# A layer's residual sum made by PE with an identity product in the output projection's bank and copied out by ScalarE, instead of added by VectorE

## The chip, the cores and the metric

The kernel runs on one core of a Trainium2 chip. The metric is the device time of one execution in microseconds (us), here the median of three runs. Engines are named as in the profile: PE is TensorE, DVE is VectorE, ACT is ScalarE, POOL is GpSimd, SP is SyncE, whose queue issues the transfers. PEld is the weight load of PE.

## What is computed

The input is 16 sequences of 512 tokens with 128 channels. Three blocks follow one another: half of a mixture of experts, a state-space block of four layers, half of a mixture of experts again.

```
x = x + 0.5 * moe(layernorm(x))          # 8 experts, width 344, top 2 of 8
x = x + mamba4(layernorm(x))
x = x + 0.5 * moe(layernorm(x))

mamba4(h):  for l in 0..3:
    xn = rmsnorm(h) * norm_w[l];  xp, z = split(xn @ Win[l])
    xc = silu(causal_conv4(xp) + conv_b);  dt, B, C = split(xc @ Wx[l])
    delta = softplus(dt @ Wdt[l] + bdt)
    state_t = exp(delta_t * A) * state_(t-1) + (delta_t * xc_t) * B_t     # 256 channels, 16 states
    y = (sum over states of state * C + xc * Dp) * silu(z)
    h = h + y @ Wblk[l]                  # the residual sum of this change
  return h @ Wout + bout
```

All of it is f32.

## The kernel before

**Tiling.** A tile is 128 partitions by 512 tokens of one sequence. The residual `h_sb` of a sequence is one such tile, channels on partitions, with four slots. The 256 inner channels are two blocks, each of them four units (j = 0..3) of four tiles: 32 scan tiles for a layer of a sequence. Such a pair of layer and sequence is called a phase, and there are 64.

**The order of work.** All engines walk over the same list of ticks t, and on each engine the instructions stand in the order of the ticks at which tables place them (`CORE`, `PREP`, `POST`, `FFN_AT`, `START`, `END`). A tick is only a place in the order: an engine goes on as soon as its semaphore waits allow. 128 ticks are a round (in the code a window, w), and in each round the core of one phase runs. Its parts, with the ticks of the round:

- ACT makes the decay exp(delta A) of each tile into one of three PSUM banks `dA_ps` (L556, every fourth tick: ..., 78, 82, 86, 90, 94, ...). An exponential waits until DVE is done with the tile three before it.
- POOL makes the input product of a unit (L909, 128x2048), DVE scans each tile (L720), and the product with C is made by POOL in pairs of tiles (L900, 128x1024, sixteen half-units for a phase less the five that DVE makes) or by DVE (L725, 128x512). PE sums over states (L405).
- In the same round PE, ACT and DVE do the preparation of the next phase (norm, convolution, projections, delta), the end of the phase before, and one expert in each 32 ticks. An expert is: PE spreads the gate (L414), DVE makes the gated input xs (L798), PE the gate projections (L421), ACT their silu (L583) in one burst with a table load before it and one behind it (L584), PE the up projections (L427), DVE the products (L805), PE the down projections (L434). The burst stands at tick 27 of each 32, so at ticks 27, 59, 91 and 123 of a round.
- An expert unit is two rounds long and begins at tick 22 of an even round. Its norm and router run in the 60 ticks ahead of that: DVE's statistics (L813, L819), ACT's normalization (L594), logits, POOL's difference of the two best logits (L930), ACT's exponential of it (L608), POOL's sum (L935), DVE's reciprocal (L855), POOL's product (L938).

**The bank s.** Five PSUM banks serve other work than the exponentials, and `s_ps` is the one that all of the preparation and the layer's end share. PE's `fill("s", ...)` waits until the last user of it is done. Ahead of the layer's end this is the copy of delta out of the bank (L684, tick 79), which itself waits for DVE's L787.

**The layer's end.** In the usual place (far; 55 of 64 phases) the output projection L514 stands at tick 83 of the round after the phase's core: two products (one for each block of `y_sb`) into `s_ps`. DVE's addition L749 stands at tick 91, behind the scan and in front of the product L725. The next layer's square L639 (`sq`) stands at tick 113. In the nine places where the next layer follows two rounds later, or after the fourth layer of one of the last two sequences (`POST_NEAR`), the projection is at tick 17 and the addition at 14. After the fourth layer `h_sb` goes into the output product (L523, L524).

```
POST = {"x1": 8, "wblk": 83, "h": 91, "attn": 105, "x2": 105}
POST_NEAR = {"x1": -65, "wblk": 17, "h": 14, "attn": 35, "x2": 56}
```

Of the kernel before, what the change touches and what calls it, by code (L numbers as in the profile page):

```python
# [8 lines left out]
ALU = mybir.AluOpType  # L9
ACT = mybir.ActivationFunctionType  # L10
# [3 lines left out]
NBLK = 2  # L14
# [21 lines left out]
NEAR = {"dc1": 98, "dc0": 84, "sq": 14, "ms": 25, "rms": 24, "xn": 27, "xp0": 45, "conv0": 42, "xp1": 47, "conv1": 53,  # L36
        "silu_xc": 59, "z0": 69, "zc0": 60, "z1": 72, "zc1": 67, "silu_z": 91, "wx": 76, "dbc": 75, "rows": 48, "dt0": 77,
        "sp0": 77, "delta0": 84, "du0": 84, "dt1": 84, "sp1": 86, "delta1": 93, "du1": 101, "dd0": 71, "dd1": 109, "bc": 55}
POST = {"x1": 8, "wblk": 83, "h": 91, "attn": 105, "x2": 105}
POST_NEAR = {"x1": -65, "wblk": 17, "h": 14, "attn": 35, "x2": 56}  # L40
FFN_AT = {"gb": 5, "xs": 2, "g0": 5, "g1": 10, "g2": 10, "burst": 5, "u0": 10, "u1": 17, "u2": 21, "hh0": 13, "hh1": 16,
          "hh2": 21, "down": 28}
START = {"load": -130, "bn": -60, "nb": -44, "xtok": -54, "xt": -38, "xT": -47, "lg": -32, "lg_sb": -35, "mx": -32,
# [18 lines left out]
PHASE = phase_table()  # L62
# [28 lines left out]
XSLOTS, HSLOTS = 2, 4  # L91
# [41 lines left out]
def post_at(t, what):  # L133

    for near, table in enumerate((POST, POST_NEAR)):
        w, s = divmod(t - table[what], W)
        if s == 0 and w - 1 in PHASE and FEEDS_NEAR[w - 1] == near:
            return ORDER[w - 1], w - 1
    return None
# [30 lines left out]
def build(nc, x, norm_w, Win, conv_w, conv_b, conv_rows, Wx, Wdt, bdt, A_log, Dp, Wblk, Wout, bout,  # L170
          Ws, bs, Wg, Wu, Wd, out, bc_rows, x1):
    with ExitStack() as ctx:
# [16 lines left out]
        wblk_sb = sb("wblk_sb", [128, NL, NBLK, D])  # L189
# [10 lines left out]
        ident = sb("ident", [128, 128])  # L200
# [16 lines left out]
        h_sb = sb("h_sb", [128, HSLOTS, T])  # L217
# [161 lines left out]
        def _(pe):  # L379
            free = {"a": None, "b": None, "s": None}  # L380

            def fill(which, sem, value):

                if free[which] is not None:
                    pe.wait_ge(*free[which])
                free[which] = (sem, value)
                return s_ps if which == "s" else ps_of[which]
# [120 lines left out]
            def post_pe(t):  # L508
                if at := post_at(t, "wblk"):
                    k, w = at  # L510
                    ps = fill("s", h_ready, k + 1)
                    for b in range(NBLK):
                        pe.wait_ge(y_gated, 2 * k + b + 1)
                        last = pe.matmul(ps[:, :], wblk_sb[:, PHASE[w][1], b, :], y_sb[:, b, :], start=(b == 0), stop=(b == NBLK - 1))  # L514
                    last.then_inc(wblk_full, 1)
                if (at := post_at(t, "attn")) and PHASE[at[1]][1] == NL - 1:
                    k, w = at
                    n = PHASE[w][0]
                    ps = fill("s", x2_ready, n + 1)
                    pe.wait_ge(h_ready, k + 1)  # L520
                    for c in range(TB):
                        o = ps[:, c * D:(c + 1) * D]
                        pe.matmul(o, h_sb[:, n % HSLOTS, c * 128:(c + 1) * 128], wout_sb[:, :], start=True, stop=False)  # L523
                        last = pe.matmul(o, ones_row[:, :].broadcast_to([1, 128]), bout_sb[:, :], start=False, stop=True)  # L524
                    last.then_inc(attn_full, 1)
# [19 lines left out]
        def _(act):  # L545
# [69 lines left out]
            def end_act(t):  # L615
# [6 lines left out]
                if (f := UNIT_OF.get(t - E * PERIOD - END["h"])) is not None and FFN[f][1] == 1:  # L622
# [3 lines left out]
                        act.wait_ge(attn_full, n - HSLOTS + 1)  # L626
                    act.activation(h_sb[:, n % HSLOTS, :], s_ps[:, :], ACT.Copy).then_inc(hin_ready, 1)

            def prep_act(t):
                if at := prep_at(t, "sq"):  # L630
                    k, w = at
# [63 lines left out]
            for t in range(FIRST, LAST):  # L695
                if t == FFN[0][0] + PERIOD:
                    act.wait_ge(w_scan, 16 * SCAN_LOADS)
                    act.activation(a_sb[:, :, :, :, :], a_sb[:, :, :, :, :], ACT.Exp).then_inc(aprep, 1)
                    act.wait_ge(aprep, 1)
                    act.activation(a_sb[:, :, :, :, :], a_sb[:, :, :, :, :], ACT.Copy, scale=-1.0).then_inc(aprep, 1)  # L700
                    for l in range(NL):
                        act.activation(win_sb[:, l, :], win_sb[:, l, :], ACT.Copy, scale=normw_sb[:, l:l + 1]).then_inc(aprep, 1)
                        act.activation(win0_sb[:, l, :], win0_sb[:, l, :], ACT.Copy, scale=normw_sb[:, l:l + 1]).then_inc(aprep, 1)
                    act.wait_ge(aprep, 2 + 2 * NL)
                core_act(t)
                burst_act(t)
                start_act(t)
                end_act(t)
                prep_act(t)

        @block.vector
        def _(dve):
# [29 lines left out]
                    dve.tensor_tensor(y_sb[:, b, :], zs_sb[:, par, b, :], y_ps[:, :], ALU.mult).then_inc(y_gated, 1)  # L742

            def post_dve(t):
                if at := post_at(t, "h"):
                    k, w = at
                    n = PHASE[w][0]
                    dve.wait_ge(wblk_full, k + 1)
                    dve.tensor_tensor(h_sb[:, n % HSLOTS, :], h_sb[:, n % HSLOTS, :], s_ps[:, :], ALU.add).then_inc(h_ready, 1)  # L749
                if (at := post_at(t, "x2")) and PHASE[at[1]][1] == NL - 1:  # L750
                    n = PHASE[at[1]][0]
                    dve.wait_ge(attn_full, n + 1)
                    dve.wait_ge(x_back[n % XSLOTS], 16 * (n // XSLOTS + 1))
                    xr = xr_sb[:, x_slot(2, n)]
                    dve.tensor_tensor(xr, xr, s_ps[:, :].rearrange("p (k d) -> p k d", k=TB), ALU.add).then_inc(x2_ready, 1)
# [279 lines left out]
```

## Time and profile before

| what | value |
| --- | --- |
| median of 3 runs | 4565.08 us (4559.62 to 4566.4) |
| the profiled execution | span 4554.2 us from its first to its last instruction; the page gives no other time for it |
| instructions | 48397 |
| busy: POOL, DVE, PE, ACT | 4093.5, 4047.9, 3939.2, 3342.2 us |
| mean granted clock of PE | 0.951 of full speed |
| chain that ended last | POOL 41%, issue 16%, DVE 14%, PE 12%, ACT 8%, DMA 3% |

The span is 10.9 us below the median of the runs. Busy times are sums over the whole span. The page's row of 40 slices shows POOL at 0 to 5 tenths in the first three slices and 6 and 0 in the last two, and at 9 tenths in every slice between.

### The profile page before, as it was taken

Reading aid. Unit: us, or ns where it says so; the run is one execution under the profiler, and the core shown is the slowest. Engines: PE = TensorE matmul, PEld = TensorE weight load, DVE = VectorE, ACT = ScalarE, POOL = GpSimd, SP = SyncE. Lnnn points to the kernel's source line nnn. Section 1 sums busy time; section 2 is a strip of 40 time slices with the busy share of each in tenths; the row PEclk is TensorE's granted clock in tenths of the full one; section 3 lists DMA queues with packets and bytes.
Section 4 is the critical chain, followed back from the end, with each engine's and each line's share of the span. In section 5 each row is a group of like instructions: output and inputs, shape, how many; then the busy total and the mean of one; then the engine's idle time right before and its main releaser. Section 6 shows DMA issues by size and latency. Waiting matters only on the chain.

```text
span 4554.2 us, 48397 instructions
## 1 busy us (share of the span) xinstructions
PE 3939.2 (86%) x11712; PEld 1280.3 (28%) x11712; DVE 4047.9 (89%) x5505; ACT 3342.2 (73%) x5047; POOL 4093.5 (90%) x1804
## 2 busy tenths in 40 slices
PE   7886777998999999899998999999899989678769
PEld 2221222232322323232232323223232323122223
DVE  2668898999999999999999999999999999889963
ACT  4566776777777777777778777777777777667734
POOL 0559999999999999999999999999999999999960
PEclk9897887999999999999999999999999999789969
DMA  2233544354434444544454445444444554444410
GB/s 72 61 78 95 115 106 98 85 118 110 97 87 112 107 93 99 114 104 96 98 112 96 97 101 119 95 97 101 112 92 89 117 113 91 101 99 95 99 41 5
DMA packets 154562, 434.46 MB, mean 95 GB/s; under 512 B 16429, under 2 KB 53230, under 8 KB 153903
## 3 DMA queue, kind: packets, MB, share of 16 engines
q1 hardware_dynamic: 154287, 431.36, 41.4%
q8 instruction: 103, 1.69, 0.2%
q14 instruction: 172, 1.41, 0.1%
HBM read 150.28 MB, written 12.58 MB: 36 GB/s over the span
## 4 chain that ended last, share of the span: by engine, by line
POOL 41%; issue 16%; DVE 14%; PE 12%; ACT 8%; DMA 3%; SPq 2%; DVEq 0%; ACTq 0%; POOLq 0%
POOL work L909 21%; POOL work L900 19%; DVE work L720 5%; DVE dA_ps L720 4%; SPq L363 2%; PE d_ps L434 2%; PE s_ps L481 2%; DVE work L725 2%; DMA bc_sb<-bc_rows 2%; ACT sg_sb L583 2%; ACT L583 1%; PE b_ps L427 1%; ACT dA_ps L556 1%; DMA dd_sb<-dd_src 1%; ACT L584 1%
## 5 line engine op out<-in xcount | busy, mean ns | idle before, releaser
L909 POOL TENSOR_TENSOR work<-dd_sb,bc_sb 128x2048 f32<-128x2048 f32 x512 | 2319.6, 4531 | 72.4 <-DMA dd_sb<-dd_src 72.2
L556 ACT ACTIVATE dA_ps<-dd_sb,a_sb 128x512 f32<-128x512 f32 x2048 | 1369.2, 684 | 643.1 <-DVE work L725 542.9
L900 POOL TENSOR_TENSOR work<-work,bc_sb 128x1024 f32<-128x1024 f32 x704 | 1655.9, 2359 | 35.1 <-DVE work L720 34.7
L720 DVE TENSOR_TENSOR_SCAN work<-dA_ps,work 128x512 f32<-128x512 f32 x1408 | 1646.7, 1203 | 40.7 <-POOL work L909 32.0
L720 DVE TENSOR_TENSOR_SCAN dA_ps<-dA_ps,work 128x512 f32<-128x512 f32 x640 | 780.9, 1220 | 10.9 <-ACT dA_ps L556 5.1
L434 PE MATMUL d_ps<-sg_sb,wd_sb 128*128 128x512 f32 (+1 forms) x1536 | 721.0, 601 | 18.8 <-DVE sg_sb L805 18.8
L405 PE MATMUL y_ps<-work,sel_sum 128*32 128x512 f32 x4096 | 580.3, 640 | 81.9 <-POOL work L900 53.7
L421 PE MATMUL a_ps<-xT_sb,wg_sb 128*128 128x512 f32 (+1 forms) x768 | 439.5, 655 | 87.1 <-ACT sg_sb L583 80.7
L421 PE MATMUL b_ps<-xT_sb,wg_sb 128*128 128x512 f32 (+1 forms) x768 | 434.5, 648 | 92.2 <-ACT sg_sb L583 87.8
L725 DVE TENSOR_TENSOR work<-dA_ps,bc_sb 128x512 f32<-128x512 f32 x640 | 435.8, 681 | 8.3
L427 PE MATMUL a_ps<-xs_sb,wu_sb 128*128 128x512 f32 (+1 forms) x768 | 412.2, 619 | 20.7 <-DVE sg_sb L805 16.2
L427 PE MATMUL b_ps<-xs_sb,wu_sb 128*128 128x512 f32 (+1 forms) x768 | 411.8, 618 | 13.4 <-DVE sg_sb L805 13.3
L434 PEld LDWEIGHTS d_ps<-sg_sb,wd_sb 128*128 128x128 f32 (+1 forms) x1536 | 279.3, 190 | 422.2 <-issue 352.7
L583 ACT ACT_TABLE_LOAD x256 | 328.4, 1283 | 85.8 <-PE d_ps L434 81.6
L805 DVE TENSOR_TENSOR sg_sb<-sg_sb,b_ps 128x512 f32<-128x512 f32 (+1 forms) x384 | 259.3, 675 | 139.8 <-PE b_ps L427 138.5
L584 ACT ACT_TABLE_LOAD x270 | 346.4, 1283 | 4.9
L805 DVE TENSOR_TENSOR sg_sb<-sg_sb,a_ps 128x512 f32<-128x512 f32 (+1 forms) x384 | 258.9, 674 | 84.5 <-PE a_ps L427 84.2
L583 ACT ACTIVATE sg_sb<-a_ps 128x512 f32<-128x512 f32 (+1 forms) x384 | 227.7, 593 | 59.4 <-PE a_ps L421 57.7
L583 ACT ACTIVATE sg_sb<-b_ps 128x512 f32<-128x512 f32 (+1 forms) x384 | 227.7, 593 | 58.5 <-PE b_ps L421 56.6
L481 PE MATMUL s_ps<-xn_pad,wconv_sb 128*128 128x512 f32 x512 | 248.9, 631 | 3.0 <-DVE xn_pad L763 2.2
L405 PEld LDWEIGHTS y_ps<-work,sel_sum 128*32 128x32 f32 x4096 | 83.0, 110 | 497.3 <-issue 359.2
L497 PE MATMUL s_ps<-dbc_sb,wdt_sb 97*128 97x512 f32 x256 | 149.5, 667 | 66.8 <-ACT dd_src L684 59.9
(116 smaller groups left out, 3823.6 us busy)
## 6 DMA issues: line engine op xcount, KB each, us to landing
dd_sb<-dd_src SPq DMA_DIRECT2D x512, 512.0 KB, 8.5
bc_sb<-bc_rows SPq DMA_DIRECT2D x256, 512.0 KB, 5.8
xr_sb<-in_L_attn_x SPq DMA_DIRECT2D x16, 256.0 KB, 3.3
bc_rows<-dbc_sb SPq DMA_DIRECT2D x128, 32.0 KB, 1.7
x<-xr_sb SPq DMA_DIRECT2D x16, 256.0 KB, 3.6
xr_sb<-x SPq DMA_DIRECT2D x16, 256.0 KB, 2.9
out<-xr_sb SPq DMA_DIRECT2D x16, 256.0 KB, 2.3
wg_sb<-in_L_ffn_Wg SPq DMA_DIRECT2D x1, 1376.0 KB
```

The costliest lines, as they stand in the source:

```text
L405: last = pe.matmul(y_ps[SEL * c:SEL * (c + 1), :], sel_sum[:, :], work[:, g % RING, c % 2, :], start=(j == 0), stop=(j == NJ - 1))
L421: pe.matmul(ps[0:fn, :], wg_sb[:, e, f0:f0 + fn], xT_sb[:, f % 2, :], start=True, stop=True).then_inc(g_full, 1)
L427: pe.matmul(ps[0:fn, :], wu_sb[:, e, f0:f0 + fn], xs_sb[:, :], start=True, stop=True).then_inc(u_full, 1)
L434: last = pe.matmul(d_ps[:, :], wd_sb[0:fn, e, ft, :], sg_sb[0:fn, ft, :], start=(e == 0 and ft == 0), stop=(e == E - 1 and ft == NFT - 1))
L556: act.activation(dA_ps[:, g % NDA, :], dd_sb[:, b, c, 0, :], ACT.Exp, scale=a_sb[:, l, b, j, c:c + 1]).then_inc(dA_ready, 1)
L583: act.activation(sg_sb[0:fn, ft, :], ps_of[job_bank(E * f + e, 1 + ft)][0:fn, :], ACT.Silu).then_inc(sg_ready, 1)
L584: act.preload_act_table_set(EXP_LN)
L720: dve.tensor_tensor_scan(dA if on_dve(i) else tile, dA, tile, 0.0, ALU.mult, ALU.add).then_inc(scanned, 1)
L725: dve.tensor_tensor(work[:, (g // 2) % RING, g % 2, :], dA_ps[:, g % NDA, :], bc_sb[:, (i // NG) % NJ, 0, :], ALU.mult).then_inc(dve_prod, 1)
L805: dve.tensor_tensor(sg_sb[0:fn, ft, :], sg_sb[0:fn, ft, :], ps_of[job_bank(E * f + e, 4 + ft)][0:fn, :], ALU.mult).then_inc(hh_ready, 1)
L900: pool.tensor_tensor(work[:, g % RING], work[:, g % RING], bc_sb[:, j, 0, :].unsqueeze(1).broadcast_to([128, 2, T]), ALU.mult).then_inc(po ...
L909: pool.tensor_tensor(work[:, g % RING:g % RING + 2].rearrange("p h c t -> p (h c) t"), dd_sb[:, b, :, 1, :], bc_sb[:, j, 1, :].unsqueeze(1 ...
```

## The change

PE puts a third product in front of the two of the output projection: the identity (`ident`, which is there already for transposes) times the old `h_sb`, accumulated in the same bank. ACT then copies the bank over the slot of `h_sb`. DVE's addition is gone. The place of the step moves from tick 91 to 85 in the usual places, so on ACT between the exponentials of ticks 82 and 86, and from 14 to 9 in the near ones; within a tick `post_act` comes behind the other parts of ACT and in front of the preparation.

```diff
-POST = {"x1": 8, "wblk": 83, "h": 91, "attn": 105, "x2": 105}
-POST_NEAR = {"x1": -65, "wblk": 17, "h": 14, "attn": 35, "x2": 56}
+POST = {"x1": 8, "wblk": 83, "h": 85, "attn": 105, "x2": 105}
+POST_NEAR = {"x1": -65, "wblk": 17, "h": 9, "attn": 35, "x2": 56}
...
                     ps = fill("s", h_ready, k + 1)
+                    pe.matmul(ps[:, :], ident[:, :], h_sb[:, PHASE[w][0] % HSLOTS, :], start=True, stop=False)
                     for b in range(NBLK):
                         pe.wait_ge(y_gated, 2 * k + b + 1)
-                        last = pe.matmul(ps[:, :], wblk_sb[:, PHASE[w][1], b, :], y_sb[:, b, :], start=(b == 0), stop=(b == NBLK - 1))
+                        last = pe.matmul(ps[:, :], wblk_sb[:, PHASE[w][1], b, :], y_sb[:, b, :], start=False, stop=(b == NBLK - 1))
                     last.then_inc(wblk_full, 1)
...
+            def post_act(t):
+                if at := post_at(t, "h"):
+                    k, w = at
+                    act.wait_ge(wblk_full, k + 1)
+                    act.activation(h_sb[:, PHASE[w][0] % HSLOTS, :], s_ps[:, :], ACT.Copy).then_inc(h_ready, 1)
...
                 end_act(t)
+                post_act(t)
                 prep_act(t)
...
             def post_dve(t):
-                if at := post_at(t, "h"):
-                    k, w = at
-                    n = PHASE[w][0]
-                    dve.wait_ge(wblk_full, k + 1)
-                    dve.tensor_tensor(h_sb[:, n % HSLOTS, :], h_sb[:, n % HSLOTS, :], s_ps[:, :], ALU.add).then_inc(h_ready, 1)
```

## Rows read from the trace of the kernel before

**Rows 1.** The page: busy us by engine; POOL's costliest group (busy, mean ns, idle before).

```profile
PE 3939.2 (86%) x11712; PEld 1280.3 (28%) x11712; DVE 4047.9 (89%) x5505; ACT 3342.2 (73%) x5047; POOL 4093.5 (90%) x1804
...
L909 POOL TENSOR_TENSOR work<-dd_sb,bc_sb 128x2048 f32<-128x2048 f32 x512 | 2319.6, 4531 | 72.4 <-DMA dd_sb<-dd_src 72.2
```

**Rows 2.** Windows view: stretch, length; busy PE, PEld, DVE, ACT, POOL; clock, DMA.

```profile
1000.00:3400.00 2400.00, 2194.18 (x6721) 717.64 (x6720) 2306.84 (x3146) 1885.95 (x2877) 2346.39 (x1035) 1.00 0.45 101
```

**Rows 3.** Waits of POOL, 1000 to 3400 us: us in total, times, longest.

```profile
POOL work L900 <- DVE work L720: 16.0, 21, 1.3
POOL wt_sb L938 <- DVE wt_sb L855: 14.0, 19, 1.1
```

**Rows 4.** Waits of DVE, the same stretch.

```profile
DVE sg_sb L805 <- PE b_ps L427: 50.4, 74, 2.9
```

**Rows 5.** Timeline of POOL: start, us, instruction, idle before it and its releaser.

```profile
590.73 2.35 POOL L900 TENSOR_TENSOR work<-work,bc_sb 128x1024 f32<-128x1024 f32 x1 [1.26 <-DVE work L720]
...
1890.58 2.36 POOL L900 TENSOR_TENSOR work<-work,bc_sb 128x1024 f32<-128x1024 f32 x1 [1.26 <-DVE work L720]
...
3855.00 2.36 POOL L900 TENSOR_TENSOR work<-work,bc_sb 128x1024 f32<-128x1024 f32 x1 [1.25 <-DVE work L720]
```

**Rows 6.** Timeline of ACT at the router's step.

```profile
1785.32 0.21 ACT L608 ACTIVATE wt_sb<-wt_sb 128x4 f32<-128x4 f32 x1 [0.34 <-POOL wt_sb L930]
```

**Rows 7.** Timeline of ACT, even round at 1829 to 1842 us.

```profile
1830.25 0.60 ACT L684 ACTIVATE dd_src<-s_ps 128x512 f32<-128x512 f32 x1 [0.59 <-DVE dd_src L787]
1830.74 1.39 ACT L556 ACTIVATE dA_ps<-dd_sb,a_sb 128x512 f32<-128x512 f32 x2
1834.53 0.69 ACT L556 ACTIVATE dA_ps<-dd_sb,a_sb 128x512 f32<-128x512 f32 x1 [2.40 <-DVE work L725]
1835.24 1.28 ACT L583 ACT_TABLE_LOAD   x1
...
1838.31 0.59 ACT L583 ACTIVATE sg_sb<-b_ps 88x512 f32<-88x512 f32 x1 [0.69 <-PE b_ps L421]
...
1840.22 1.91 ACT L556 ACTIVATE dA_ps<-dd_sb,a_sb 128x512 f32<-128x512 f32 x3
```

**Rows 8.** Timeline of DVE, the same stretch.

```profile
1836.08 0.67 DVE L749 TENSOR_TENSOR h_sb<-h_sb,s_ps 128x512 f32<-128x512 f32 x1
1836.66 0.68 DVE L725 TENSOR_TENSOR work<-dA_ps,bc_sb 128x512 f32<-128x512 f32 x1
1837.26 2.33 DVE L720 TENSOR_TENSOR_SCAN work<-dA_ps,work 128x512 f32<-128x512 f32 x2
1839.51 0.66 DVE L805 TENSOR_TENSOR sg_sb<-sg_sb,a_ps 128x512 f32<-128x512 f32 x1
1840.19 0.69 DVE L805 TENSOR_TENSOR sg_sb<-sg_sb,b_ps 128x512 f32<-128x512 f32 x1
1840.94 1.23 DVE L720 TENSOR_TENSOR_SCAN dA_ps<-dA_ps,work 128x512 f32<-128x512 f32 x1
```

**Rows 9.** Timeline of PE (matmuls), the same stretch.

```profile
1830.90 1.98 PE L514 MATMUL s_ps<-y_sb,wblk_sb 128*128 128x512 f32 x4 [0.61 <-ACT dd_src L684]
...
1833.13 1.12 PE L421 MATMUL b_ps<-xT_sb,wg_sb 128*128 128x512 f32 x2
...
1837.18 1.09 PE L421 MATMUL b_ps<-xT_sb,wg_sb 128*88 128x512 f32 x2 [0.88 <-ACT sg_sb L583]
```

**Rows 10.** Line L514, all of the span: PE's idle time before it until, us, times.

```profile
  ACT dd_src L684: 133.6, 110
```

**Rows 11.** Waits of ACT, 1000 to 3400 us.

```profile
ACT wt_sb L608 <- POOL wt_sb L930: 12.5, 17, 1.3
```

**Rows 12.** Timeline of PE at two near places.

```profile
229.99 1.98 PE L514 MATMUL s_ps<-y_sb,wblk_sb 128*128 128x512 f32 x4 [0.69 <-ACT xT_sb L605]
...
4212.80 1.13 PE L514 MATMUL s_ps<-y_sb,wblk_sb 128*128 128x512 f32 x2 [1.21 <-DVE y_sb L742]
```

**Rows 13.** Windows view of a third near place, columns as in rows 2.

```profile
4012.29:4016.07 3.78, 3.78 (x8) 1.04 (x4) 3.28 (x4) 0.20 (x1) 3.78 (x2) 0.50 0.27 101
```

## The prediction

> **What bounds the kernel now.** I read the page's busy times first. POOL and DVE are nearly equal over the span, and PE is close behind [rows 1]. An average over filling, steady work and emptying can't say which one sets the pace, so the next view is the windows view of a steady stretch: there POOL works 2346.39 of 2400 us, DVE 2306.84, PE 2194.18 and ACT only 1885.95 [rows 2]. POOL is at 97.8%. Its waits in the same stretch show what keeps it from 100%: its products (L900) wait 21 times for a DVE scan, 16.0 us, and its router step (L938) waits 19 times for DVE's reciprocal, 14.0 us [rows 3]. So POOL sets the pace, and now and then it is itself held up by a chain in which DVE comes last.
>
> The next question is what makes DVE late. DVE's own waits answer it: DVE waits for PE's up-projection, 50.4 us in 74 waits, and next to nothing for POOL [rows 4]. DVE isn't simply full; PE makes it late. I therefore followed the chain back through the timelines, starting from the longest of POOL's waits.
>
> POOL waits 1.26 us at 1890.58 for a scan. That is the tenth of the sixteen half-unit products of a phase, in an odd round (a round is 128 ticks). There are 26 odd rounds between the rows at 590.73 and 3855.00, and this same product waits over 0.1 us in 23 of them, up to 1.27 us [rows 5]. The chain behind such a wait begins some 105 us earlier, at POOL's router step L930, for which ScalarE waits (0.34 us in the row at 1785.32) [rows 6]; in between it runs through ACT, PE and DVE alone. It crosses the even round's tick 83 to 100, the place of the change, like this. ACT's exponential at 1834.53 waits for DVE's product L725 (2.40 us); behind it stand the table load, two silus, the wait for PE, a third silu, the second load and the exponentials of 1840.22 [rows 7], each starting where the one before ends. DVE's scan at 1840.94 can't start before the first of these exponentials is done [rows 8]. The old addition at 1836.08 lies in front of this scan too, but the way through ACT ends at the same time (the scan starts 0.03 us after the exponential ends at 1840.91). Two routes tie here: one over ACT's burst, and one over DVE's queue with the addition in it.
>
> **The change part by part.** *Removed:* 64 additions on VectorE, 0.67 us each. In the queue one costs 0.58 us, the distance from 1836.08 to the start at 1836.66 [rows 8]: 37 us of DVE's issue time in all, 0.58 per round.
>
> *Added on PE:* one f32 product of 128x128 by 128x512 in each phase. L514's two such products are four passes, 1.98 us, and one such product as a pair of passes is 1.12 (the row at 1833.13, same shape), so two more passes cost 0.86 us [rows 9]. The bank comes free with ACT's copy L684, and in 55 of 64 phases this copy is what L514 waits for (110 waits, weight load and product, 133.6 us) [rows 10]; the new product stands behind that same release, so it isn't hidden. In the even round: PE ends at 1830.90 + 1.98 + 0.86 = 1833.74.
>
> *Added on ACT:* a copy out of PSUM. From the start of such a copy (1830.25) to the next exponential's start (1830.74) is 0.49 us [rows 7]. There is room for it: ACT idles 2.40 us at this place. But the copy is not last in line. It is put between the exponentials of ticks 82 and 86, and it waits for PE. What is queued behind it: the exponential of tick 86, which used to run at once at about 1831.44 (the second of the pair), that of tick 90 (1834.53), and the burst. Worked out: PE's end 1833.74, plus 0.04 for the signal (PE's pair from 1837.18 ends at 1838.27 and ACT starts at 1838.31 [rows 7, 9]), copy at 1833.78; exponential of tick 86 at 1834.27; that of tick 90 another 0.62 later (three exponentials take 1.91 us, so (1.91 - 0.67)/2) at 1834.89 instead of 1834.53. **The burst starts 0.36 us later** in every round that has expert work.
>
> *Downstream of the burst.* First silu +0.36, so PE's product at 1837.18 (released by that silu) at 1837.54, the third silu, the second load and the exponential of 1840.22 at 1840.58, the scan at 1841.30. DVE, freed of 0.58, would be at its first L805 at 1838.93, but its inputs come from PE at 0.36 later than before, so DVE waits there. The gain is lost at this wait, and the chain is 0.36 longer. PE's own extra 0.86 us are absorbed earlier: PE idled 0.88 us before 1837.18 [rows 9]. The scans of ticks 95 and 99 began at 1837.26 and would be wanted at 1836.68 [rows 8]; their exponential is done at 1834.96. So no scan starves, with 1.7 us to spare.
>
> *Odd rounds.* Here DVE also carries the normalization's statistics and its queue is the later one, so the 0.58 us count for DVE, or the 0.36 count against ACT; but both end at the anchor: ACT waits for POOL's L930 in 17 of 19 cases, 12.5 us in all [rows 11]. Nothing of either reaches POOL unless ACT's reserve there, 0.34 us at the least of the usual cases, is used up. I take zero; the reserve and the 0.36 are so close that a loss here is one of the rivals.
>
> *Steady sum.* In each double round, the way from L930 to the tenth product is 0.36 us longer and POOL waits that much more. I count the 23 odd rounds that have such a wait, and nothing for the three in which POOL arrives later than the chain: 23 x 0.36 = **+8.3 us**. Bounds: from below -0.58 (DVE's way alone decides) to above 0.86 (all of PE's addition passes on) per double round.
>
> At one place the Trainium skill speaks for the change: Perfetto Trace Analysis, section Optimizing Scalar/DVE Operations, holds that when DVE is saturated, moving work to Scalar may make sense. DVE's 96% in the steady stretch looks like that case [rows 2]; by that rule the sum would be a gain of up to 0.58 us for each of 55 phases, 32 us. The waits of DVE for PE [rows 4] speak against its premise here, and my sum goes by these.
>
> *The edges.* Where few phases overlap, latency counts, and POOL waits for the load of dd_sb (72.2 us) [rows 1]. At 229.99 [rows 12] L514 waits for ACT's copy of xT: the added 0.86 is on the way, and the copy (0.60 for 0.67) gives 0.07 back: +0.8. At 4012.29 the granted clock is 0.50, the lower of its two levels, the four passes take 3.78 us [rows 13], and nothing is waited for between them: two more are +1.7, less 0.07: +1.6. At 4212.80 and two like it the second half waits 1.21 us for y_sb [rows 12], which hides the identity product, and DVE's queue is 0.58 shorter on a chain that waits for DVE: -0.6 each, -1.7 in all. The other four near places (half clock or a bank wait against a shorter queue) I put at +0.5 together. Edges **+1.2 us**.
>
> Sum +8.3 + 1.2 = +9.5. The profiled span is 4554.2 us and becomes 4563.7; the runs' median is 10.9 us above the span, and I carry that over: 4565.08 + 9.5 = **4574.6 us**, +0.21%.
>
> **The rivals.** *Faster (DVE's way decides).* If the even round's chain is limited by DVE's queue and ACT's delay has reserve, each of the 23 waits shrinks by up to 0.58 us: -13 us, 4552. For it: the addition lies on one of the two tied routes, and DVE is last before each POOL wait. Against it: the distances in [rows 7] have no slack between 1834.53 and 1840.22. It decides if the copy starts by 1833.42 (1834.53 - 0.62 - 0.49), so if PE's added product costs 0.50 us or less instead of 0.86. This is also what the skill's rule gives in sign. *No change.* POOL's waits grow in the chain but slack that I haven't seen takes 0.36 us, since the chain is 105 us long; then only the edges are left: 4566. Against: at each step that I followed the next instruction starts where the one before ends. *Every round pays.* The odd rounds use up ACT's 0.34 us in front of L608 and add to L938's wait as well: 52 x 0.36 = 18.7, with the edges 4585. For: the reserve is just the size of the delay. Against: a wait at L938 moves POOL and so shortens the following wait at the tenth product. *Starved scans.* If PE came to the product over 1.7 us later, DVE's scans would stand still for each 0.1 us beyond; this happens only in the few rounds at half clock, and would give 4590 or more.
>
> **How the numbers follow.** Forecast 0.46 (alone 4569 to 4580), faster 0.13, no change 0.22, every round pays 0.15, starved scans 0.04. The range runs from 4560, which leaves out the faster case, to 4586, which takes in the case of every round; outside are some 0.17. A measurement of this kernel tells from no change what exceeds about 0.2%, 9.1 us, so the line is at 4574.2: a little over half of the forecast's chance lies above it (0.25), with the last two 0.44 for slower; 0.43 for the same; 0.13 for faster.
>
> **What the profile after would show.** L514 with six passes and 2.84 us. ACT's copy starting 2.9 us after L514's start. The burst's table load 0.36 us later behind L684 than before (5.35 against 4.99 us from 1830.25 to 1835.24). A new wait of DVE's L805 for PE's a_ps of 0.6 us in even rounds. POOL's wait at the tenth product 0.3 to 0.4 us longer in most odd rounds, and ACT's wait at L608 in the 0.34 us cases gone. DVE's busy time 43 us less, ACT's 38 more. The prediction is wrong in its steady part if the table load comes at its old distance, or if POOL's waits for L720 fall below 34.7 us in total.

## The result, and the profile after

| kernel | median us | lowest to highest | runs |
| --- | --- | --- | --- |
| before | 4562.35 | 4557.17 to 4566.4 | 4 |
| after | 4599.16 | 4595.44 to 4602.7 | 4 |

The ratio is 1.0083, with a 95% interval of 1.0068 to 1.0097: slower by 36.8 us, where the prediction said 9.5 and its range ended at 4586. The direction was right, the size was not.

The page of the kernel after, its busy times and POOL's product with C, which answer to [rows 1], and to the products of [rows 5]:

```profile
PE 4007.3 (87%) x11840; PEld 1305.3 (28%) x11840; DVE 4019.7 (87%) x5441; ACT 3375.3 (73%) x5111; POOL 4097.1 (89%) x1804
...
L903 POOL TENSOR_TENSOR work<-work,bc_sb 128x1024 f32<-128x1024 f32 x704 | 1658.8, 2363 | 66.4 <-DVE work L728 65.6
```

DVE works 28.2 us less, ACT 33.1 and PE 68.1 us more. POOL works as long as before (4097.1 against 4093.5), in a span that is 46.8 us longer. So no engine became the bound by its work; POOL waits more. The windows view of the steady stretch says the same beside [rows 2] (same columns), where POOL had 2346.39:

```profile
1000.00:3400.00 2400.00, 2209.07 (x6706) 723.79 (x6705) 2260.37 (x3079) 1875.52 (x2867) 2314.99 (x1022) 0.99 0.44 101
```

POOL's waits in that stretch (us in total, times, longest), beside [rows 3]:

```profile
POOL work L903 <- DVE work L728: 37.8, 47, 1.5
POOL wt_sb L941 <- DVE wt_sb L858: 13.6, 19, 1.1
POOL rs_sb L920 <- DVE mv_sb L822: 10.9, 18, 0.6
```

The first was 16.0 us in 21 waits. The third is not among those of before at all: POOL's step in the normalization now waits for DVE's statistics. Both point to DVE, so the next view is DVE's own waits, beside [rows 4]:

```profile
DVE sg_sb L808 <- PE b_ps L427: 60.2, 90, 2.4
DVE y_sb L750 <- PE s_ps L515: 27.8, 36, 0.8
```

The second line names what the prediction doesn't have. L750 is DVE's gated product, y times silu(z), which writes `y_sb`. It waits for the output projection, PE's L515, which reads `y_sb`. The code says why:

```
if k > 0:
    dve.wait_ge(wblk_full, k)     # the group of the phase before has read y_sb
dve.tensor_tensor(y_sb[:, b, :], zs_sb[:, par, b, :], y_ps[:, :], ALU.mult).then_inc(y_gated, 1)
```

`wblk_full` has two waiters: the step that takes the sum out of the bank, and this product of the next phase, which must not overwrite `y_sb` while PE still reads it. For block 0 it stands at tick 87, four ticks behind the projection. The line's view, its idle time before it over the whole span (us, times), first of before, then of after:

```profile
  PE s_ps L514: 3.7, 4
```

```profile
  PE s_ps L515: 50.1, 55
```

55 is the number of phases with the usual (far) place. The timelines show one such place. Before, PE's group ended at 1830.90 + 1.98 = 1832.88 [rows 9], and DVE's queue of before stood like this (start, us, instruction):

```profile
1832.38 0.73 DVE L736 SCALAR_TENSOR_TENSOR y_ps<-xc_sb,dp_sb,y_ps 128x512 f32<-128x512 f32 x1
1833.14 0.69 DVE L742 TENSOR_TENSOR y_sb<-zs_sb,y_ps 128x512 f32<-128x512 f32 x1
1833.75 0.69 DVE L725 TENSOR_TENSOR work<-dA_ps,bc_sb 128x512 f32<-128x512 f32 x1
```

The product came 0.26 us behind the group's end, without a wait. After, the same place; PE first:

```profile
1851.25 1.12 PE L512 MATMUL s_ps<-h_sb,ident 128*128 128x512 f32 x2 [0.62 <-ACT dd_src L691]
1852.22 1.88 PE L515 MATMUL s_ps<-y_sb,wblk_sb 128*128 128x512 f32 x4
```

then DVE:

```profile
1852.73 0.73 DVE L744 SCALAR_TENSOR_TENSOR y_ps<-xc_sb,dp_sb,y_ps 128x512 f32<-128x512 f32 x1
1854.23 0.69 DVE L750 TENSOR_TENSOR y_sb<-zs_sb,y_ps 128x512 f32<-128x512 f32 x1 [0.77 <-PE s_ps L515]
1854.84 0.68 DVE L733 TENSOR_TENSOR work<-dA_ps,bc_sb 128x512 f32<-128x512 f32 x1
1855.44 0.68 DVE L801 TENSOR_TENSOR xs_sb<-xT_sb,a_ps 128x512 f32<-128x512 f32 x1
```

and ACT, beside [rows 7]:

```profile
1850.60 0.60 ACT L691 ACTIVATE dd_src<-s_ps 128x512 f32<-128x512 f32 x1 [0.59 <-DVE dd_src L790]
1851.10 0.69 ACT L557 ACTIVATE dA_ps<-dd_sb,a_sb 128x512 f32<-128x512 f32 x1
1854.13 0.60 ACT L634 ACTIVATE h_sb<-s_ps 128x512 f32<-128x512 f32 x1 [2.35 <-PE s_ps L515]
1854.63 0.69 ACT L557 ACTIVATE dA_ps<-dd_sb,a_sb 128x512 f32<-128x512 f32 x1
1855.62 0.69 ACT L557 ACTIVATE dA_ps<-dd_sb,a_sb 128x512 f32<-128x512 f32 x1 [0.30 <-DVE work L733]
1856.33 1.28 ACT L584 ACT_TABLE_LOAD   x1
```

The group ends at 1854.10. ACT's copy starts 0.03 us later, as worked out. DVE's product starts 0.13 later, and has then stood for 0.77. That number could have been read before the change: with 0.13 for the signal, the release was at 1833.01 and the product at 1833.14, a reserve of 0.13; a group 0.86 longer gives a wait of 0.73. The trace of before even holds the case itself. In one of the four waits of the gated product, PE's mean granted clock over the group was 0.66 and the four passes took 2.88 us, about as long as the six of the new group (PE, then DVE, both of before):

```profile
656.96 2.88 PE L514 MATMUL s_ps<-y_sb,wblk_sb 128*128 128x512 f32 x4 [2.28 <-ACT dd_src L684]
```

```profile
659.97 0.69 DVE L742 TENSOR_TENSOR y_sb<-zs_sb,y_ps 128x512 f32<-128x512 f32 x1 [0.81 <-PE s_ps L514]
```

Here too the product starts 0.13 us behind the group's end, and it has stood for 0.81.

What is behind it in DVE's queue moves too: the product L733, for which ACT's exponential of tick 90 waits (0.30 us), and the expert's gated input L801. The table load is now 1856.33 - 1850.60 = 5.73 us behind the copy of delta, not 4.99 as before nor 5.35 as predicted. That holds for all 36 such places between 1000 and 3400 us: 5.72 or 5.73 in each of them, against 4.98 or 4.99 before. In an odd round it goes the same way; there DVE's statistics are in the queue as well, and POOL's own step waits for them (DVE, then POOL):

```profile
1918.57 0.69 DVE L750 TENSOR_TENSOR y_sb<-zs_sb,y_ps 128x512 f32<-128x512 f32 x1 [0.77 <-PE s_ps L515]
...
1921.27 0.38 DVE L822 BATCH_NORM_AGGREGATE mv_sb<-bn_sb 128x2 f32<-128x6 f32 x4
```

```profile
1921.74 0.23 POOL L920 TENSOR_SCALAR rs_sb<-mv_sb 128x4 f32<-128x4 f32 x1 [0.58 <-DVE mv_sb L822]
```

**Where the time lies.** POOL's tenth half-unit product of a phase is again the anchor [rows 5]. Its first and last of the steady part, after:

```profile
593.97 2.37 POOL L903 TENSOR_TENSOR work<-work,bc_sb 128x1024 f32<-128x1024 f32 x1 [1.26 <-DVE work L728]
...
3899.87 2.36 POOL L903 TENSOR_TENSOR work<-work,bc_sb 128x1024 f32<-128x1024 f32 x1 [1.25 <-DVE work L728]
```

From the one to the other are 25 double rounds: 3305.9 us, against 3855.00 - 590.73 = 3264.3 before. That is 41.6 of the span's 46.8 us, 1.66 per double round; filling takes 3.2 more and emptying 1.9. Of the 41.6 us, POOL's waits for DVE's scans make 25.1 (23.5 us in 33 waits before, 48.6 in 62 after), its new wait at L920 makes 14.3 (24 waits), and one for DVE's L847 makes 3.1 (from 1.7 to 4.8); small differences take back 0.9. The tenth product itself waits over 0.1 us in 25 of the 26 odd rounds instead of 23, 31.2 us in all instead of 21.7. That is 9.5 us, under a quarter: most of the loss lies at other products and at L920.

The spans differ by 46.8 and the medians by 36.8. In every run whose span is known the time is the span plus 1.7 to 1.8 us, not 10.9, so the profiled execution of before took 6.5 us less than its median and that of after 3.5 more; sums of waits from these two traces carry this difference too.

### The profile page after: what moved, and what is told of

Its sections match the earlier page's. It is cut to its first block, busy times and chain, and to the rows that moved or that the text cites. A ratio compares the mean times of both kernels' runs of the same rounds, so it can differ in the third digit from the quotient of the medians.

```text
span 4601.0 us, 48589 instructions
## 1 busy us (share of the span) xinstructions
PE 4007.3 (87%) x11840; PEld 1305.3 (28%) x11840; DVE 4019.7 (87%) x5441; ACT 3375.3 (73%) x5111; POOL 4097.1 (89%) x1804
## 4 chain that ended last, share of the span: by engine, by line
DVE 26%; PE 18%; issue 18%; ACT 17%; POOL 16%; DMA 1%; SPq 1%; DVEq 0%; ACTq 0%; POOLq 0%
POOL work L912 9%; DVE work L728 8%; DVE dA_ps L728 8%; POOL work L903 6%; ACT dA_ps L557 4%; DVE work L733 4%; ACT L584 3%; ACT sg_sb L584 3%; ACT L585 3%; PE d_ps L434 2%; PE s_ps L481 2%; PE s_ps L515 2%; PE a_ps L421 2%; PE b_ps L427 2%; PE b_ps L421 2%
## 5 line engine op out<-in xcount | busy, mean ns | idle before, releaser
L903 POOL TENSOR_TENSOR work<-work,bc_sb 128x1024 f32<-128x1024 f32 x704 | 1658.8, 2363 | 66.4 <-DVE work L728 65.6
L728 DVE TENSOR_TENSOR_SCAN work<-dA_ps,work 128x512 f32<-128x512 f32 x1408 | 1647.7, 1205 | 41.5 <-POOL work L912 27.4
L405 PE MATMUL y_ps<-work,sel_sum 128*32 128x512 f32 x4096 | 586.3, 646 | 80.6 <-POOL work L903 47.4
L733 DVE TENSOR_TENSOR work<-dA_ps,bc_sb 128x512 f32<-128x512 f32 x640 | 437.2, 683 | 10.2
L405 PEld LDWEIGHTS y_ps<-work,sel_sum 128*32 128x32 f32 x4096 | 83.4, 111 | 503.3 <-issue 357.2
```

The lines of the kernel that those rows point to most:

```text
L405: last = pe.matmul(y_ps[SEL * c:SEL * (c + 1), :], sel_sum[:, :], work[:, g % RING, c % 2, :], start=(j == 0), stop=(j == NJ - 1))
L728: dve.tensor_tensor_scan(dA if on_dve(i) else tile, dA, tile, 0.0, ALU.mult, ALU.add).then_inc(scanned, 1)
L733: dve.tensor_tensor(work[:, (g // 2) % RING, g % 2, :], dA_ps[:, g % NDA, :], bc_sb[:, (i // NG) % NJ, 0, :], ALU.mult).then_inc(dve_prod, 1)
L903: pool.tensor_tensor(work[:, g % RING], work[:, g % RING], bc_sb[:, j, 0, :].unsqueeze(1).broadcast_to([128, 2, T]), ALU.mult).then_inc(po ...
```

## The experiments

Every kernel is timed against the kernel before on the same chip. Before had 4562.35 us (4 runs) beside after, 4563.03 (27 runs) beside kernels 1 to 4 and 4565.15 (21 runs) beside kernels 5 to 8; the table has the kernels in the order of their numbers. A loss "against before" is taken with the one beside the kernel. In all of them the wait of DVE's gated product and the distance from the copy of delta to the table load are read at the same places as above. Theory A is this wait; B is the prediction's, ACT's copy in front of the exponentials; C is that PE's two passes cost wherever they stand.

| kernel | median us | ratio and interval | wait for `y_sb`: us, times | load behind copy, us |
| --- | --- | --- | --- | --- |
| after | 4599.16 | 1.0083, 1.0068 to 1.0097 | 50.1, 55 | 5.73 |
| identity last, own release | 4574.63 | 1.0024, 1.0015 to 1.0034 | 4.0, 4 | 5.34 |
| identity first, DVE copies | 4594.57 | 1.0066, 1.0051 to 1.0081 | 50.7, 55 | 5.72 |
| ACT copies, no identity | 4566.23 | 1.0006, 0.9997 to 1.0016 | 3.9, 4 | 4.99 |
| identity last, copy at tick 87 | 4570.37 | 1.0013, 1.0003 to 1.0022 | 4.0, 4 | 4.99 |
| identity last, waits for all | 4601.20 | 1.0084, 1.0068 to 1.0099 | 50.6, 55 | 5.72 |
| identity last, DVE copies | 4568.87 | 1.0007, 0.9998 to 1.0016 | 3.7, 4 | 4.99 |
| after, gated product at tick 89 | 4621.17 | 1.0124, 1.0109 to 1.0140 | 8.1, 4 | 5.34 |
| before, gated product at tick 89 | 4568.28 | 1.0009, 1.0000 to 1.0018 | 1.0, 1 | 3.75 |

**1. The identity product last, and a release of its own.** The same work on every engine as after. Only `y_sb` is released as early as before the change.

```diff
-                    pe.matmul(ps[:, :], ident[:, :], h_sb[:, PHASE[w][0] % HSLOTS, :], start=True, stop=False)
                     for b in range(NBLK):
                         pe.wait_ge(y_gated, 2 * k + b + 1)
-                        last = pe.matmul(..., start=False, stop=(b == NBLK - 1))
-                    last.then_inc(wblk_full, 1)
+                        last = pe.matmul(..., start=(b == 0), stop=False)
+                    last.then_inc(y_read, 1)
+                    pe.matmul(ps[:, :], ident[:, :], h_sb[...], start=False, stop=True).then_inc(wblk_full, 1)
...
-                        dve.wait_ge(wblk_full, k)
+                        dve.wait_ge(y_read, k)
```

> The changed kernel, but PE makes the identity product behind the two products of y_sb instead of in front, and a semaphore of its own after those two tells DVE that y_sb has been read; ACT's copy still waits for all three. Theory A (the cost is DVE's gated product, which waits 50.1 us in all in the changed kernel because the longer group holds y_sb): that wait falls back to under 8 us, the later burst of my prediction stays (0.36 us in even rounds), 4568 to 4576 us. Theory B (the cost is ACT's copy, standing in front of exponentials and burst): nothing changes, 4595 to 4603. Theory C (PE is full and two more passes per phase cost what they take, wherever they stand): the same 4595 to 4603.

Measured 4574.63 us, in theory A's range. 25.2 of the 36.8 us are gone with the wait, and what is left, +11.6 us, is near what the prediction had worked out for the whole change (+9.5). The gated product (line, shapes, count, busy and mean, idle before) in after and here:

```profile
L750 DVE TENSOR_TENSOR y_sb<-zs_sb,y_ps 128x512 f32<-128x512 f32 x128 | 88.0, 687 | 52.6 <-PE s_ps L515 50.1
```

```profile
L751 DVE TENSOR_TENSOR y_sb<-zs_sb,y_ps 128x512 f32<-128x512 f32 x128 | 87.9, 687 | 8.2 <-PE s_ps L515 4.0
```

The kernel also shows the predicted course of the even round, undisturbed. Its timeline on ACT, PE and DVE:

```profile
1838.70 0.60 ACT L692 ACTIVATE dd_src<-s_ps 128x512 f32<-128x512 f32 x1 [0.59 <-DVE dd_src L791]
...
1842.23 0.60 ACT L635 ACTIVATE h_sb<-s_ps 128x512 f32<-128x512 f32 x1 [2.35 <-PE s_ps L517]
1842.73 1.30 ACT L558 ACTIVATE dA_ps<-dd_sb,a_sb 128x512 f32<-128x512 f32 x2
1844.04 1.28 ACT L585 ACT_TABLE_LOAD   x1
```

```profile
1839.35 1.98 PE L515 MATMUL s_ps<-y_sb,wblk_sb 128*128 128x512 f32 x4 [0.62 <-ACT dd_src L692]
1841.17 1.02 PE L517 MATMUL s_ps<-h_sb,ident 128*128 128x512 f32 x2
```

```profile
1841.59 0.69 DVE L751 TENSOR_TENSOR y_sb<-zs_sb,y_ps 128x512 f32<-128x512 f32 x1
...
1848.04 0.69 DVE L809 TENSOR_TENSOR sg_sb<-sg_sb,a_ps 128x512 f32<-128x512 f32 x1 [0.45 <-PE a_ps L428]
```

The load stands 1844.04 - 1838.70 = 5.34 us behind the copy of delta (predicted 5.35), and DVE stands 0.45 us for the up projection (predicted 0.6).

**2. The identity product first, and DVE copies the bank out at the old ticks 91 and 14.** So this is PE's half of the change without ACT's.

```diff
-POST = {"x1": 8, "wblk": 83, "h": 85, "attn": 105, "x2": 105}
-POST_NEAR = {"x1": -65, "wblk": 17, "h": 9, "attn": 35, "x2": 56}
+POST = {"x1": 8, "wblk": 83, "h": 91, "attn": 105, "x2": 105}
+POST_NEAR = {"x1": -65, "wblk": 17, "h": 14, "attn": 35, "x2": 56}
...
-                    act.activation(h_sb[:, PHASE[w][0] % HSLOTS, :], s_ps[:, :], ACT.Copy).then_inc(h_ready, 1)
...
+                    dve.tensor_copy(h_sb[:, PHASE[w][0] % HSLOTS, :], s_ps[:, :]).then_inc(h_ready, 1)
```

> PE's half of the change alone: identity product first in the group as in the changed kernel, but DVE copies the bank out at the old ticks 91 and 14, and ACT gets nothing. Theory A: DVE's gated product waits as long as in the changed kernel (about 50 us), and DVE isn't relieved of 0.58 us per round either, so at least as slow as the changed kernel: 4599 to 4635 us. Theory B: as the kernel before, 4560 to 4567. Theory C: 4595 to 4603.

Measured 4594.57 us, +31.5: nearly all of the loss, with nothing moved to ACT. Theory B falls as the main cause. But the time is also below theory A's range, which began at 4599: the expectation took the lost relief of DVE for a cost, and the kernel is 5.3 us nearer to before than after is (31.5 against 36.8). Theory C's range began at 4595, so this kernel doesn't tell C from A; kernels 5 and 6 do. The same row:

```profile
L743 DVE TENSOR_TENSOR y_sb<-zs_sb,y_ps 128x512 f32<-128x512 f32 x128 | 87.9, 687 | 53.2 <-PE s_ps L515 50.7
```

The load is at 5.72 here too. So in after it is this wait that sets the distance; ACT, with its copy and the exponential behind it, stands idle for 0.30 us until DVE's L733 lets it go on.

**3. ACT's copy without the identity product.** The residual sum is left out; this is ACT's half, and DVE's relief, alone.

```diff
-                    pe.matmul(ps[:, :], ident[:, :], h_sb[:, PHASE[w][0] % HSLOTS, :], start=True, stop=False)
...
-                        last = pe.matmul(..., start=False, stop=(b == NBLK - 1))
+                        last = pe.matmul(..., start=(b == 0), stop=(b == NBLK - 1))
```

> ACT's half of the change alone: the group has the two products of y_sb as before, and ACT copies the bank out at ticks 85 and 9. This leaves out the residual sum (h becomes y @ Wblk), so it is no version to use; it shows what ACT's place costs and what DVE's relief is worth. Theory A: no wait of the gated product beyond the 3.7 us of the kernel before, PE's group ends 1.98 us after its start, the copy is through early enough that the exponential of tick 90 isn't late: between 4545 and 4563 us. Theory B: ACT's copy costs even so, 4580 to 4600. Theory C: 4555 to 4565.

Measured 4566.23 us: the interval (0.9997 to 1.0016) holds no change, and not the gain of 13 us of the rival "faster". Theory A had asked for 4545 to 4563 and C for 4555 to 4565, so both ranges were missed: the relief was expected to bring something. The windows view of the steady stretch:

```profile
1000.00:3400.00 2400.00, 2195.49 (x6708) 717.07 (x6708) 2288.76 (x3109) 1900.77 (x2907) 2343.23 (x1033) 0.99 0.45 101
```

DVE works 18 us less than in [rows 2] and POOL doesn't work a microsecond more. Half of the 18 us shows up again as DVE's wait for PE's up projection, which was 50.4 us in 74 waits [rows 4]:

```profile
DVE sg_sb L807 <- PE b_ps L427: 59.9, 92, 3.0
```

So moving the step from DVE to ACT gains nothing here. What DVE's 0.58 us per round would bring by themselves, and what ACT's copy takes, this kernel doesn't tell apart.

**4. As 1, with the copy at tick 87 instead of 85,** so behind the exponential of tick 86.

```diff
-POST = {"x1": 8, "wblk": 83, "h": 85, "attn": 105, "x2": 105}
+POST = {"x1": 8, "wblk": 83, "h": 87, "attn": 105, "x2": 105}
```

> As the first (identity product last, y_sb signalled on its own), and ACT's copy moved from tick 85 to 87, so behind the exponential of tick 86 and in front of that of tick 90, at which ACT used to idle 2.4 us. If A explains most and my prediction's 0.36 us per double round the rest, both are gone: the burst's table load is again 4.99 us behind L684's start, and DVE's queue is 0.58 us shorter: 4545 to 4563 us, the kernel before or a little better. Theory B (ACT's copy costs in any place): 4580 to 4600. Theory C: 4595 to 4603.

Measured 4570.37 us, with the load back at 4.99. That is above the expected 4545 to 4563: 7.3 us stay though the burst isn't late any more. It is 4.3 us less than kernel 1 by the medians and 5.8 by the means, so the prediction's term, the burst 0.36 us later, has the right sign. Its size is the least certain of those given here: the two intervals overlap from 1.0015 to 1.0022, the runs of this kernel go from 4557.5 to 4575.2, and the predicted 8.3 isn't excluded.

**5. The identity product last, but the gated product waits for the whole group.** Against kernel 1 nothing differs but what the wait counts.

```diff
-                    last.then_inc(y_read, 1)
...
-                        dve.wait_ge(y_read, k)
+                        dve.wait_ge(wblk_full, k)
```

> The identity product is last in PE's group, as in e1_identity_last, but DVE's gated product again waits for the end of the whole group. This takes the order of the products apart from the wait. Theory A (the wait): all of e1's gain is lost, y waits of some 50 us, the burst's table load 5.7 us behind L684's start, 4594 to 4603 us. If the order on PE were what helped (the accumulation begins with y_sb, weights come sooner): 4570 to 4578.

Measured 4601.20 us, ratio 1.0084: the whole loss is back, with the wait:

```profile
L749 DVE TENSOR_TENSOR y_sb<-zs_sb,y_ps 128x512 f32<-128x512 f32 x128 | 88.0, 687 | 53.1 <-PE s_ps L515 50.6
```

Kernels 1 and 5 differ by 26.6 us (24.5 when each is taken against before on its own chip). It is the wait, not the order of the products or the place of the identity's passes on PE, and neither theory B nor C as first stated: both have no place for a difference between these two kernels.

**6. The identity product last with its own release, and DVE copies at ticks 91 and 14.** PE's two more passes alone. Against kernel 1:

```diff
-POST = {"x1": 8, "wblk": 83, "h": 85, "attn": 105, "x2": 105}
-POST_NEAR = {"x1": -65, "wblk": 17, "h": 9, "attn": 35, "x2": 56}
+POST = {"x1": 8, "wblk": 83, "h": 91, "attn": 105, "x2": 105}
+POST_NEAR = {"x1": -65, "wblk": 17, "h": 14, "attn": 35, "x2": 56}
...
-                    act.activation(h_sb[:, PHASE[w][0] % HSLOTS, :], s_ps[:, :], ACT.Copy).then_inc(h_ready, 1)
...
+                    dve.tensor_copy(h_sb[:, PHASE[w][0] % HSLOTS, :], s_ps[:, :]).then_inc(h_ready, 1)
```

> PE's extra passes alone: the identity product last, y_sb signalled on its own in front of it, and DVE copies the bank out at the old ticks 91 and 14; ACT has nothing of it. What is left of the change is two more passes of PE in each phase. Theory A with PE's passes hidden in its waits: 4561 to 4567 us. Theory C in a weak form (the passes cost a few us as PE comes later to the experts' products; the fourth experiment less the third gave 4.1 us by the medians): 4565 to 4570.

Measured 4568.87 us, no change that the interval (0.9998 to 1.0016) can tell. Against kernel 2, which copies on DVE as well but makes the product wait, it is 27.8 us less, each taken against before. The windows view:

```profile
1000.00:3400.00 2400.00, 2225.90 (x6794) 730.60 (x6794) 2307.04 (x3150) 1890.09 (x2876) 2346.83 (x1034) 1.00 0.45 101
```

PE works 32 us more than in [rows 2] and POOL's 2346.83 is that of before, so in this execution the steady part has room for the passes. Theory C as first stated (4595 to 4603) falls. Its weak form, that the passes cost a few us, isn't excluded: its range (4565 to 4570) holds the result, theory A's (4561 to 4567) doesn't, and the interval reaches up to 7.3 us.

**7. After, with the gated product of block 0 at tick 89 instead of 87.** The opposite of removing the wait: let DVE do other work in front of it.

```diff
-CORE = {"exp": -10, "scan": -1, "dbu": -3, "dve_prod": 0, "pool_prod": 21, "sum": 30, "y0": 87, "y1": 8}
+CORE = {"exp": -10, "scan": -1, "dbu": -3, "dve_prod": 0, "pool_prod": 21, "sum": 30, "y0": 89, "y1": 8}
```

> The changed kernel with one table entry moved: DVE's skip and gated product of block 0 stand at tick 89 instead of 87, so behind the product L733 (tick 88) and the expert's xs product (tick 88), for which ACT and PE wait. The wait for y_sb's release then falls behind them in DVE's queue. Theory A: y waits near zero, the exponential of tick 90 isn't held up by DVE, what stays is the 0.36 us of ACT's order and PE's passes: 4566 to 4577 us. Theory B or C: 4595 to 4603.

Measured 4621.17 us, so 22 us above after, or 19.2 when each is taken against before on its own chip; the expectation was wrong. The wait that it names is gone (8.1 us in 4 places), but another has taken its place. DVE's two rows and the timeline at the same stretch:

```profile
L750 DVE TENSOR_TENSOR y_sb<-zs_sb,y_ps 128x512 f32<-128x512 f32 x128 | 87.8, 686 | 12.4 <-PE s_ps L515 8.1
L801 DVE TENSOR_TENSOR xs_sb<-xT_sb,a_ps 128x512 f32<-128x512 f32 x128 | 86.4, 675 | 97.9 <-PE a_ps L414 97.9
```

```profile
1858.36 0.69 DVE L733 TENSOR_TENSOR work<-dA_ps,bc_sb 128x512 f32<-128x512 f32 x1
1859.96 0.69 DVE L801 TENSOR_TENSOR xs_sb<-xT_sb,a_ps 128x512 f32<-128x512 f32 x1 [0.91 <-PE a_ps L414]
```

The next but one in DVE's queue, the expert's gated input, needs PE's gate spreading L414, and that stands on PE behind the same longer group: at 1854.03 in after, as the four passes end. In after, L801 on this bank idles 50.9 us in 20 waits; here 97.9 in 72. The group has a third waiter, by PE's order and not by a semaphore, and it had been covered by the second. POOL's wait at L920 grows with it, in the steady stretch from 10.9 to 18.6 us. The move does one thing more: PE's L405, which needs the bank that the gated product reads, now waits for that product, 83.1 us in 64 waits against 12.9 in 9 in after.

**8. Before, with the gated product at tick 89,** the control for 7.

```diff
-CORE = {"exp": -10, "scan": -1, "dbu": -3, "dve_prod": 0, "pool_prod": 21, "sum": 30, "y0": 87, "y1": 8}
+CORE = {"exp": -10, "scan": -1, "dbu": -3, "dve_prod": 0, "pool_prod": 21, "sum": 30, "y0": 89, "y1": 8}
```

> The control of e5: the kernel before with the same move of DVE's gate from tick 87 to 89 and nothing else. In it the gated product hardly waits (3.7 us), so if the move is worth nothing in itself: 4560 to 4567 us. If it comes out faster or slower than the kernel before by more than 3 us, e5 is to be read against this run and not against the kernel before.

Measured 4568.28 us (1.0000 to 1.0018): the move itself costs some 3 us, if anything, and the result is 1.3 above the range for "nothing". L405 waits here as in kernel 7 (84.7 us in 64 waits), but DVE's xs product L798 idles no more than before (49.9 us in 20 waits against 50.0 in 19). So about 16 us of kernel 7 (56.0 against before, less the 36.8 of after and these 3.1) come only when the move and the longer group stand together. The wait for L414 is what they have and the control hasn't; no kernel takes that wait away by itself, so this cause is read from the traces and not shown by a run. The control says something on the burst as well: its load stands 3.75 us behind the copy of delta, 1.24 earlier than before, and the kernel isn't faster.

A second buffer for `y_sb`, which would take the wait away without another semaphore, wasn't tried.

## Why the prediction was wrong

**What bounds the kernel: right in the main.** POOL paces and DVE comes last before its waits. The place was too narrow: the tenth product's wait grows by 9.5 us over the 26 odd rounds, 0.37 in each, which is just the predicted 0.3 to 0.4. That this number came true is luck, for a double round grew by 1.66 us, beyond the upper bound of 0.86 that the prediction gave, and three quarters of it lie at other products and at L920.

**The step that failed is "Added on PE".** It worked out when the group ends and followed only the step behind `h_sb` from there, which the change moves to ACT. It didn't ask who else waits for that end. The gated product of DVE waits for the same semaphore at tick 87, in code that the change doesn't touch, and had 0.13 us of reserve against 0.86 us of delay. Three pairs that differ by this wait show that it makes 24 to 28 us of the 36.8: after and kernel 1 25.2, kernels 5 and 1 24.5, kernels 2 and 6 27.8. The first and the third pair differ in the order of the products as well, and kernel 5 shows the order to be worth nothing (1.0084, after 1.0083). It came with the sentence "DVE, freed of 0.58": DVE was freed of 0.58 in a round and given a wait of 0.77 in the same ticks.

**"Odd rounds ... I take zero" failed with it.** The wait stands in every far phase, so DVE's queue is late in odd rounds as well. POOL's new wait at L920, 18 times and 10.9 us in the steady stretch, is not in the prediction. The rival "every round pays" named the odd rounds, but through ACT's L608 and with 0.36 us in each; its 4585 is short of the result, and its mechanism is not what happened. The rival "starved scans" asked for PE to be 1.7 us late, and for half clock; neither was needed.

**The ACT term had its steps right; its price stays open.** Copy 2.88 us behind the group's start (2.9 predicted), burst 0.35 us later (0.36) and a wait of 0.45 us where DVE's products need PE's a_ps (0.6): in kernel 1 each step is there. As a sum, +9.5 for steady part and edges together, against +11.6 measured for kernel 1 with an interval of 1.0015 to 1.0034, so 6.8 to 15.5 us. That the sum comes near is in part luck. Kernel 4 puts the burst's delay at 4.3 to 5.8 us instead of 8.3, and leaves 7.3 for which the prediction has only the edges' 1.2. And the tenth product, where the 8.3 was to arrive, waits 29.2 us in the same 26 rounds in kernel 1, but 27.4 in kernel 4 and 25.1 in kernel 3, where the burst isn't late (one execution each; 21.7 before, 21.6 in kernel 6). So most of the growth there goes with ACT making the copy, at either tick, and not with the burst. In kernels 3 and 6, each half alone, the medians are 3.2 and 3.7 us above before, with zero inside both intervals. Together these would make up 6.9 of the 7.3, but a difference of this size in one half can't be told from none here; this part stays open.

**The edges.** Filling, up to the tenth product of round 5, takes 3.2 us more and the end 1.9, so 5.2 in after before rounding; in kernel 1, without the wait, +2.5 and -0.6, so 1.9 against the predicted 1.2.

**The signs of being wrong didn't fire.** The prediction named two: the table load at its old distance (it came at 5.73, later than foreseen), and POOL's waits for L720 below 34.7 us (they are 65.6). Both looked for a chain shorter than predicted, none for a longer one.

**The smaller statements.** Six passes of the group, 2.85 us: as predicted (2.84). DVE's busy time -28.2 us: predicted -43, the 64 removed additions at 0.67 us each; why less is gone wasn't looked into. ACT's +33.1: predicted 38. The relief of DVE lost at a wait: so, and kernel 3 shows no gain from it even when PE's group isn't longer. The 10.9 us between span and median, carried over as if they lay around the span, were mostly the distance of the one profiled execution from the others; the time around the span is 1.7 us.

**The Trainium skill's rule** (Perfetto Trace Analysis, Optimizing Scalar/DVE Operations: when DVE is saturated, moving work to Scalar may make sense) would have given a gain of up to 32 us here. Kernel 3 moves that work alone, with DVE at 96% of the steady stretch before, and gives 1.0006 (0.9997 to 1.0016). The measurement decides: in this kernel DVE's busy share was no sign that its work set the pace.

## What to carry to other kernels

When a step gets longer, list everything that waits for its end before costing any of it: each wait on its semaphore, in code that the change leaves alone too (an operand's buffer to be overwritten is one), and what stands behind it in its own engine's order. For each, read the reserve out of the trace of before, as the start of the waiter less the end of the step; a delay larger than the smallest reserve is a new wait. Count how often it occurs: here 55 times, 50.1 us of waiting, of which 24 to 28 us reached the kernel's time. If an operand of an accumulation group is wanted back early, put the products that read it first, and release it apart from the result: here that alone was worth 25 us of 37.

## What the runs showed of the hardware

The identity product costs PE the same at the head of the group (six passes in 1851.25 to 1854.10, 2.85 us, against 1.98 for four [rows 9], so 0.87) and at its tail (in kernel 1 from the four passes' end at 1841.33 to 1842.19, so 0.86). The instructions that wait for a group's last pass don't all start at the same distance: in after ACT's copy stands 0.03 us behind it and DVE's gated product 0.13. It isn't the engine that makes the difference: before, DVE's addition that waited for the group of 229.99 [rows 12] started at 232.01, 0.04 us behind its end.
